# A transformer megakernel on one core: the lead of the attention's maxima rises at the start and falls in a last head group taken backwards

## What is computed

```python
def attn_a(x):                              # x is normalised before
    q, k, v = split(x @ W_attn)             # 16 heads of 16
    att = einsum('bhqd,bhkd->bhqk', q, k) / sqrt(16)
    att = softmax(where(causal, att, -inf))
    att = att * decay_weight_matrix(T)      # 0 where q - k >= 511
    return (einsum('bhqk,bhkd->bhqd', att, v)) @ W_proj

def attn_b(x):                              # biases, no decay, a layer norm behind it
    att = softmax(where(causal, einsum('bhtd,bhsd->bhts', q, k) / sqrt(16), -inf))
    return layernorm(einsum('bhts,bhsd->bhtd', att, v) @ Wo + bo) * gamma + beta
```

## Time and profile before

| | before |
|---|---|
| three runs | 2669.0, 2675.54, 2676.61 us |
| profiled execution | 2671.95 us, span 2670.2 us |
| PE (matmuls) busy | 2396.0 us, 90% of the span |
| PEld (weight loads) busy | 1367.6 us, 51% |
| DVE, ACT, POOL busy | 1962.1, 1499.8, 1054.0 us |
| granted TensorE clock, mean | 0.951 |
| attention a, first M to last PV | 157.7 to 1131.4 us |
| attention b, first M to last PV | 1476.6 to 2406.1 us |

### The profile page before, as it was taken

How to read it: one execution, slowest core, us unless ns; L and a number is a source line. 1 busy time by engine, 2 the same in 40 slices (tenths; PEclk the granted TensorE clock), 3 DMA queues, 4 the chain that set the end, 5 groups by cost and what they waited for, 6 DMA issues and landing times. The chain is left out here.

```text
span 2670.2 us, 43926 instructions
## 1 busy us (share of the span) xinstructions
PE 2396.0 (90%) x13600; PEld 1367.6 (51%) x13600; DVE 1962.1 (73%) x4834; ACT 1499.8 (56%) x3293; POOL 1054.0 (39%) x1274
## 2 busy tenths in 40 slices
PE   4969999999999999859996899999999999992887
PEld 2544545555454545346764455555555555532666
DVE  5677888878888888337653988888888878833887
ACT  1218677776868777614331266666666666670233
POOL 0037778788787778813211301010010110103552
PEclk8969999999999999979998699999999999996999
DMA  4684243351615330053323644261542615004210
GB/s 150 255 145 59 37 55 51 45 73 18 85 26 66 46 50 10 10 164 115 130 98 123 88 65 62 30 85 30 66 61 30 85 26 70 10 9 140 77 50 32
DMA packets 158806, 188.69 MB, mean 71 GB/s; under 512 B 65520, under 2 KB 89584, under 8 KB 157808
## 3 DMA queue, kind: packets, MB, share of 16 engines
q1 hardware_dynamic: 153840, 175.91, 33.5%
q10 hardware_dynamic: 4736, 9.96, 1.9%
HBM read 114.37 MB, written 69.99 MB: 69 GB/s over the span
## 5 line engine op out<-in xcount | busy, mean ns | idle before, releaser
L688 POOL TENSOR_TENSOR att_a_wd<-att_a_wt,decay 128x256 f32<-128x256 f32 (+3 forms) x896 | 754.4, 872 | 208.5 <-PE att_a_po L864 120.5
L718 ACT ACTIVATE att_b_wt<-att_b_ps 128x512 f32<-128x512 f32 (+3 forms) x1280 | 592.3, 540 | 325.5 <-PE att_b_ps L842 323.7
L759 DVE TENSOR_REDUCE att_a_mpart<-att_a_pm 128x1 f32<-128x512 f32 x768 | 508.8, 686 | 115.9 <-PE att_a_pm L829 110.8
L759 DVE TENSOR_REDUCE att_b_mpart<-att_b_pm 128x1 f32<-128x512 f32 x768 | 503.5, 685 | 95.4 <-PE att_b_pm L829 93.7
L829 PE MATMUL att_a_pm<-att_a_kop,att_a_qop 128*128 128x512 f32 (+3 forms) x1280 | 510.8, 425 | 45.5 <-DMA att_a_kop<-qk 19.1
L718 ACT ACTIVATE att_a_wt<-att_a_ps 128x512 f32<-128x512 f32 (+3 forms) x896 | 433.0, 511 | 207.2 <-PE att_a_ps L845 145.0
L829 PE MATMUL att_b_pm<-att_b_kop,att_b_qop 128*128 128x512 f32 (+3 forms) x1280 | 486.7, 400 | 29.7 <-DMA att_b_kop<-qk 18.4
L842 PE MATMUL att_b_ps<-att_b_qop,att_b_kop 128*128 128x512 f32 (+3 forms) x1280 | 453.9, 384 | 13.7 <-DMA att_b_qop<-att_b_mrow 9.1
L698 POOL TENSOR_SCALAR_AFFINE_SELECT att_b_wt<-att_b_wt 128x512 f32<-128x512 f32 x128 | 81.4, 636 | 837.4 <-ACT att_b_wt L718 837.4
L829 PEld LDWEIGHTS att_a_pm<-att_a_kop,att_a_qop 128*128 128x128 f32 x1280 | 237.9, 193 | 307.2 <-DVE att_a_mpart L759 139.7
L829 PEld LDWEIGHTS att_b_pm<-att_b_kop,att_b_qop 128*128 128x128 f32 x1280 | 244.9, 194 | 245.9 <-DVE att_b_mpart L759 119.3
(11 more groups left out here) (167 smaller groups left out, 2512.1 us busy)
## 6 DMA issues: line engine op xcount, KB each, us to landing
att_a_kop<-qk SPq DMA_DIRECT2D x128, 128.0 KB, 7.0
att_b_kop<-qk SPq DMA_DIRECT2D x128, 128.0 KB, 6.0
att_a_qop<-qk SPq DMA_DIRECT2D x112, 128.0 KB, 6.6
att_b_qop<-qk SPq DMA_DIRECT2D x112, 128.0 KB, 6.6
qk<-qkv_a_qk_hi SPq DMA_DIRECT2D x8, 1024.0 KB, 4.1
qk<-qkv_a_qk_lo SPq DMA_DIRECT2D x8, 1024.0 KB, 6.0
y<-att_a_y SPq DMA_DIRECT2D x32, 256.0 KB, 2.2
qk<-mid_qk_hi SPq DMA_DIRECT2D x8, 1024.0 KB, 4.3
```

Source lines behind the costliest of these rows:

```text
L688: pool.tensor_tensor(wd[:, kq % 2, j, a:z], wt[:, kq % buffers, j, a:z], keep["decay"][:, u:u + z - a], ALU.mult).then_inc(w_decayed, 1)
L718: act.activation(wt[:, kq % buffers, j, a:CH], pe_[:, n % EBANKS, 0:CH - a], ACT.Exp)\
L759: dve.tensor_reduce(mpart[:, c, piece, u:u + 1], pm[:, n % MBANKS, 0:w], AX.X, ALU.max, negate=True).then_inc(m_reduced, 1)
```

## The change

The chunk order of the last group (g = 7) becomes 3, 2, 1, 0 (`sequence`). The lead of M is no constant any more: at position `at` of the S stream it is the least of `LEAD`, `FIRST + RISE * at` and `FINAL + FALL * (8 - at)`. A second rule comes with it: ahead of an S of a chunk the plan puts M until that chunk's maxima are made and `MARGIN` = 12 more units have been placed. The list is now written in one pass:

```diff
 LEAD = {True: 0.38, False: 0.45}
+FIRST, RISE, FINAL, FALL, MARGIN = 0.25, 0.30, 0.11, 0.60, 12
...
+def sequence(g):
+    return range(NC) if g < GROUPS - 1 else range(NC - 1, -1, -1)
...
+def place(g, c):
+    return NC * g + list(sequence(g)).index(c)
...
+def lead(at, decayed):
+    ends = min(FIRST + RISE * at, FINAL + FALL * max(0.0, GROUPS - at))
+    return min(LEAD[decayed], ends)
...
-    m = spaced(m, decayed)
-    timed = []
-    for number, (lead, items) in enumerate(((0.0, e), (LEAD[decayed], m))):
-        total, position = sum(x for x, _ in items) / GROUPS, 0.0
-        for cost, item in items:
-            position += cost
-            timed.append((position / total - lead, number, len(timed), item))
-    timed += [(g + t, 2, c, ("L", g + 1, c)) for g in range(GROUPS - 1) for c, t in enumerate(FETCH)]
-    return [item for _, _, _, item in sorted(timed)]
...
+    for cost, item in e:
+        first = (item[1], item[3]) if item[0] == "S" else None
+        while count < len(m) and (m_at < e_at + lead(e_at, decayed) or first and count < made.get(first, count) + MARGIN):
+            m_cost, unit = m[count]
+            _, g, n, c, qb, j, piece = unit
+            plan.append(unit)
+            m_at, count = m_at + m_cost / m_total, count + 1
...
+            left[g, c] -= 1
+            if left[g, c] == 0:
+                plan.append(("MF", g, c))
+                made[g, c] = count
+                follow((3, ("MC", g, c)))
+                if far(c, decayed):
+                    follow((8, ("FE", g, c)), (11, ("FM", g, c)), (14, ("FT", g, c)))
...
+        while fetch and fetch[0][0] <= e_at:
+            plan.append(fetch.pop(0)[1])
+        plan.append(item)
+        e_at += cost / e_total
```

As maxima of two groups can now be under way in another chunk order, `mpart`, `fsum` and `frow` get two halves by the parity of the group, `y` and `scol` alternate by `place` in place of the chunk's number, and the counts on which engines wait are read off the list:

```diff
-        mpart = sb("mpart", [P, NC, NC, UNITS], F32)
+        mpart = sb("mpart", [P, 2, ROWS, UNITS], F32)
...
-            fsum, ffactor = (sb(n, [P, NC, NC - 2, UNITS], F32) for n in ("fsum", "ffactor"))
-            ftotal, frow = sb("ftotal", [P, NC - 2, SQUARE], F32), sb("frow", [P, NC - 2, SQUARE], F32)
+            fsum, ffactor = sb("fsum", [P, 2, NC - 1, UNITS], F32), sb("ffactor", [P, NC - 1, UNITS], F32)
+            ftotal, frow = sb("ftotal", [P, NC - 2, SQUARE], F32), sb("frow", [P, 2, NC - 2, SQUARE], F32)
...
+        MADE, TURNED, DIFFED = counts("MF"), counts("FT"), counts("FE")
+        M_COUNT, FX_COUNT, PV_COUNT = counts("M"), counts("FX"), counts("PV")
...
-                    dve.wait_ge(m_reduced, M_UNITS * g + GH * sum(TB * (a + 1) for a in range(c + 1)) + MBANKS)
+                    dve.wait_ge(m_reduced, M_COUNT[g, c] + MBANKS)
...
-                    if g > 0:
-                        dve.wait_ge(s_summed, len(FARS) * (g - 1) + n + 1)
-                    dve.transpose(frow[:, n, :], ftotal[:, n, :]).then_inc(f_turned, 1)
+                    if g > 1:
+                        dve.wait_ge(s_summed, SUMMED[g - 2, c])
+                    dve.transpose(frow[:, g % 2, n, :], ftotal[:, n, :]).then_inc(f_turned, 1)
```

More of the change, by code:

```diff
@@ L436 @@
 M_UNITS = UNITS * sum(c + 1 for c in range(NC))
-FAR_UNITS = UNITS * sum(max(0, c - 1) for c in range(NC))
+ROWS = NC * (NC + 1) // 2
 def near(c, decayed):
@@ L447, in far, with follow @@
     return range(max(0, c - 1) if decayed else 0)
-def visits_before(g, c, decayed):
-    per = [len(near(a, decayed)) for a in range(NC)]
-    return sum(per) * g + sum(per[:c])
+def sequence(g):
[5 more added lines that the diff above has]
+    return min(LEAD[decayed], ends)
 def attention_plan(decayed):
-    order = [(g, c, kb) for g in range(GROUPS) for c in range(NC) for kb in near(c, decayed)]
+    order = [(g, c, kb) for g in range(GROUPS) for c in sequence(g) for kb in near(c, decayed)]
     per_group = len(order) // GROUPS
     due = {}
-    def follow(number, j, item):
-        cost = PV_TIME if item[0] in ("PO", "PV") else 0.0
+    def follow(number, j, cost, item):
         due.setdefault((number, j) if number < len(order) else None, []).append((cost, item))
@@ L483, in attention_plan @@
         n = 0
-        for c in range(NC):
+        for c in sequence(g):
             for qb in range(TB):
@@ L499, in attention_plan @@
-    return [item for _, _, _, item in sorted(timed)]
-def spaced(m, decayed):
-    out, late = [], []
-    def follow(*items):
[L507 to L514, removed]
-        if item[0] == "M" and item[6] in far(item[3], decayed):
-            follow((1, 0.0, ("FX", *item[1:])))
-        if item[0] == "MF":
-            g, c = item[1:]
-            follow((3, 0.0, ("MC", g, c)))
-            if far(c, decayed):
-                follow((8, 0.0, ("FE", g, c)), (11, 0.0, ("FM", g, c)), (14, 0.0, ("FT", g, c)))
-    return out + [(200.0, x[2]) for x in sorted(late, key=lambda x: x[0])]
+    plan, late, made, left = [], [], {}, {(g, c): UNITS * (c + 1) for g in range(GROUPS) for c in range(NC)}
@@ L525, in attention @@
+    return plan
 def attention(nc, name, decayed, keep, dram):
@@ L669, in _ @@
                     sp.dma_start(rows.rearrange("j (t k i) -> k (j t) i", t=TB, k=P // SQUARE),
[L670 removed]
+                                 inverse[0:P:SPREAD, side(g, c), :]).then_inc(s_out[side(g, c)], 16)
             for i in range(2):
@@ L801, in _ @@
                     c = item[2]
-                    dve.wait_ge(s_in[c % 2], S_DMAS * (2 * g + c // 2 + 1))
-                    dve.wait_ge(s_out[c % 2], 16 * (2 * g + c // 2 + 1))
+                    dve.wait_ge(s_in[side(g, c)], S_DMAS * (place(g, c) // 2 + 1))
+                    dve.wait_ge(s_out[side(g, c)], 16 * (place(g, c) // 2 + 1))
                     if c in FARS:
@@ L813, in _ @@
             pe.sem_inc(pv_done, buffers)
+            begun = set()
             for item in PLAN:
```

133 lines of the change are left out of this document (75 added, 58 removed).

## The result

| | before | after |
|---|---|---|
| median (runs) | 2674.69 us (10) | 2693.31 us (10) |
| lowest to highest | 2669.0 to 2677.36 | 2687.89 to 2704.65 |
| profiled execution, its span | 2671.95, 2670.2 us | 2694.58, 2692.9 us |
| attention a, first M to last O | 974.0 us | 996.4 us |
| attention b, first M to last O | 929.8 us | 929.2 us |

The ratio is 1.0071, with a 95% interval of 1.0058 to 1.0085: the change costs 18.6 us, by the medians. In the two profiled executions attention a pays all of it, and b comes out even.

A forecast was written before the change was run, and what follows sets the result against it. PE, busy 97 and 98% in the mixtures, was taken as the bound, by block start times. Terms summed to +17.9 us in a, -4.7 in b, with clock +13.8: 2672 + 14 = 2686 us, range 2663 to 2702.

The forecast's parts named there:

- (1): Openings: first S comes earlier after the first M, -8.3 us in a and -15.6 us in b.
- (2): M that leave the openings, 22 in a and 32 in b, cost PE time in the mixture: +4.6 and +6.4 us.
- (3): Tails: 34 and 52 S instead of 44 and 72 in a and b, -1.5 and -2.5 us.
- (4): Runs of M ahead of an S, paced by DVE and the row's DMA chain: +23 us in a, +16.9 in b.
- (6): New wait in b: loads L(1,0) stand ahead of chunk 1's row DMAs on SP, +1.5 us, between 0 and 4.
- (5): PE's waits for chunk rows in b go, by twelve M of margin and an earlier last row: -11.4 us.
- (7): Lower clock after long runs of M: +0.6 us in all, near b's opening, between 0 and 4.5.
- Rival B: Faster: PE not full in the mixture, moved M fill bubbles, runs cost half; 2655 us; under 2667 chance 0.15.
- The rival reading of PE by its weight loads: Mixtures: with PEld busy only 51 and 52%, the 54 moved M cost nothing and the sum is 11 us lower.
- Rival A: Runs cost only their issue, rows being in time: 2667 us, partly up to 2677; chance 0.29 with Rival B's mixed cases.
- rival C: Clock stays low through 13 S after a run, or chunk 3's loads are late in b: 2694 to 2701 us, chance 0.06.
- D: Groups 1 to 6 keep their order; difference lies in first group, last and end; middle changes over 5 us mean something missed.

The follow-up runs named there:

- the fastest kernel: The change with both last groups in rising order, no falling lead, b's lead 0.48 and rise 0.45, next group's loads issued earlier: 2641.07 us, 0.987.
- spread out: The change with a's lead cap growing from 0.38 to 0.50 over group 6, so the runs of 21 and 23 M vanish: 2673.96 us, 0.9994.
- the lead alone: The kernel before with one number changed, attention b's constant lead 0.48 in place of 0.45: 2674.67 us, 0.9997.

## Why the prediction was right, and where it was off

The forecast was +13.8 us and 2686; the runs gave +18.6 and 2693.3, inside the range. The main mechanism was the forecast one: the two long runs in a's last group make the loss, and the shorter openings are paid back. The forecast's terms, put to the groups in which they fall, beside the profiled executions:

| us | forecast | measured |
|---|---|---|
| a, group 0: (1), (2) | -3.7 | -0.7 |
| a, groups 1 to 5 | 0 | +1.0 |
| a, groups 6 and 7: (3), (4) | +21.6 | +22.1, of it 4.8 clock |
| b, group 0: (1), (2), (4), (6), one wait of (5) | +0.3 | 0.0 |
| b, groups 1 to 5: (4) +1, (5) -7.3 | -6.3 | -2.0 |
| b, groups 6 and 7: (3), (4), (5) | +1.2 | +1.4 |
| clock (7) | +0.6 | in the rows above |

Measured this way the attentions differ by 21.8 us, the two profiled spans by 22.7 and the medians by 18.6. The forecast also counted from the profiled execution, 2672, which lies 2.7 us under the median of ten.

Some of the agreement is luck. Without the clock a's groups 6 and 7 lost 17.3 us, where (3) and (4) had 21.6, and the clock, which (7) had nearly left out, made up for it with 4.8. In a's group 0 and in b's middle the sum was 3 and 4 us too hopeful.

**(1)** was right: first S in a 27.7 us after its first M and in b 23.2, with 27.7 and 22.7 forecast, both ended by the row's DMA. (The two times given for a, 185.4 and 194.0, are 8.6 apart and not 8.3, a slip of 0.3.) **(2)** was right in sign; in b it has the right size together with the short runs of (4). b gives its 15 us back by the end of group 0: at the four chunks' ends it is 12.6, 7.5, 1.4 and 0.0 us ahead. Rival B is out with this: the moved M and the runs together cost what block start times gave. In a the gain is down to 0.5 us by the second chunk, and 3 us more are lost than forecast. It isn't the clock, which is as low over the first 4 us with S before as after:

```profile
194.00:198.00 4.00, 4.00 (x14) 3.42 (x13) 2.88 (x7) 3.15 (x8) 2.31 (x2) 0.50 1.08 117
...
186.00:190.00 4.00, 4.00 (x11) 3.28 (x12) 2.28 (x6) 1.80 (x4) 2.49 (x2) 0.50 1.08 134
```

The first is of before, the second of after. From the first S to the end of the second chunk a takes 63.4 us for 55.4, with nearly all of the 22 moved M in it: almost 0.4 us for each, where (2) took 0.21. PE waits 3.0 us there for banks that FX gives back, for 1.4 before. Why the rest is dearer stays open.

The rival reading of PE by its weight loads can be weighed in part. In the fastest kernel's middle of b PE is busy 679.92 of 680 us and PEld 364.99, 54%. Its groups shortened by 3.3 us, of which 2.7 are PE's idle time (16.4 us over 6.07 groups). Matmul starts and idle time told what these edits could win. The Trainium skill (Perfetto Trace Analysis, the note at its head) calls matmul busy time a bad metric and the LDWEIGHTS share a good one; read so, 46% would be left. No run here won more than these 3 us in 112, and none was made to find out how much of the 46% could be had.

**(3)** The tails are 33.0 and 29.3 us for 31 and 33 forecast, 2 longer and 4 shorter. **(4)** The runs are 11.9 and 13.9 us long, where I had 13.7 and 14.1, and PE would have paid 4.4 and 4.8 for their M: +7.5 and +9.1 for +9.3 each. The timeline of DVE in the first has

```profile
1030.26 0.20 DVE L820 STREAM_TRANSPOSE att_a_mrow<-att_a_mneg 128x32 f32<-128x32 f32 x1
```

7.4 us after the run's start, where my sum of backlog, reductions and three narrow M had 9.4; from there to the S it took 4.5, for 4.35. Rival A is out: spread out, the two runs gave back 17.7 us, and PE waited for the row at the end of both.

**(5) is the step that failed.** "Twelve M of margin ... take these away": they did not. In the kernel after, the waits view of b from 1560 us on has

```profile
PEld att_b_ps L867 <- DMA att_b_qop<-att_b_mrow: 8.7, 9, 2.1
PE att_b_ps L867 <- DMA att_b_qop<-att_b_mrow: 6.3, 9, 1.8
```

where the earlier trace rows had 9.2 and 2.2. The last chunk's 2.2 us did go. But groups 0 to 6 still wait once each at the first S of chunk 3, now 0.6 to 2.2 us; in groups 1 to 6 that makes 6.0 us for 8.1. It is the main reason why b's mixture is 31 us longer and not 24. Nine M and five narrow S lie between MC and that S for six and six before. At 0.23 us for an M, that is some 0.6 us more cover, and in groups 1 to 3 it took about that off waits of 1.2. I had compared counts and not times, though the chain's time stood in (4). Most middle groups did shorten by about 1.0, and the five together by 2.0, since one of them holds the longer stretch at the lower clock. Nor were the 7.3 us there to be had from the rows: with the lead alone PE waits for none, and the groups stay at 112, for then the banks that DVE gives back are late.

**(7) was mis-sized.** The clock fell to half in both runs and cost about 5 us (4.8 in place), where I took 0.6, placed near b's opening, with an upper end of 4.5. I had also expected PE to be two thirds idle in the runs; it was busy for about two thirds, in part because its M took longer at the lower clock. It was half of rival C: the lower level lasted over one and a half blocks of S, not three. The Trainium skill (TensorE: Matmul & The Clock Gate, Part 1) has the clock set by how busy PE has been, and by that alone I had named the upper end as the value. The traces agree with it: 0.50 behind ten microseconds in which PE was busy for 6.7, and 1.00 throughout with the added matmuls.

**(6)** was small: the first S of chunk 1 in b's group 0 waits 0.4 us for its row, with 1.5 forecast. **D** held, since a's groups 1 to 5 moved by 1.0 us and b's by 2.0 in all.

## What to carry to other kernels

Where a strictly ordered queue must produce something by a deadline, look at the longest bunch that the deadline rule makes, and price it as the longer of the chain behind it (here reduction, transpose, four small DMAs) and the pace of the engine that takes its results, and not as its instructions. Add what the clock does behind it, and behind a mere wait too. A shorter opening is worth only as much as the moved work finds free time. An engine's idle time in the steady state, here 16 of 680 us, was worth more than both ends: the fastest kernel is 33 us faster than the one before, with rows made earlier, no bunches and loads issued where no small DMA stands behind them. Taking one of these waits away alone gave nothing, because the next one took its place. A simple merge can hide a priority: move what frees a buffer together with what fills it.

## What the runs showed of the hardware that was not expected

In the first long run no wait of PE was longer than 1.6 us, and PE was busy for 6.7 of the ten us from 1020 on; the granted clock was then 0.50, 1.2 in place of 2.4 GHz, from 1030 to 1040, and the pairs of S in it took 1.22 us for 0.73. Useless matmuls in the gaps of both runs kept the clock at 1.00 and made the kernel 6.9 us faster, 4.8 of them in place.

In b's middle groups, single waits of 1.3 to 2.3 us for a row stood right before stretches of 3.4 or 6.8 us at 0.50 in the traces of seven kernels, while other waits of 1.3 to 1.5 us had none behind them. The group with such a stretch is 2 to 5 us longer than its neighbours, more than the wait itself.

Moving the 28 fetches of a chunk (eight loads each) in each attention on SP's queue by at most 0.08 of a group, with no byte more or less, took 1.2 us off each middle group of b and 5.8 us off the kernel.
